# Feed-forward stage: the rows of z become bf16 whole numbers on ScalarE before TensorE transposes them

## The reference

```python
def h_bitlinear(x, w):
    xq = act_quant(fwht(x))      # Hadamard rotation, then each row rounded to whole numbers of 8 bits times its scale
    wq = weight_quant(w)         # weights rounded to -1, 0, 1 times one scale
    return jnp.einsum('bsh,oh->bso', xq, wq)
gate = h_bitlinear(hidden_states, w_gate)      # 512 -> 2048
up = h_bitlinear(hidden_states, w_up)          # 512 -> 2048
return h_bitlinear(jax.nn.silu(gate) * up, w_down)   # 2048 -> 512
```

## Time and profile before

| what | us |
|---|---|
| median of three executions | 3221.47 (3221.32 to 3223.74) |
| the profiled execution, device time | 3223.19 |
| its span in the profile | 3221.4 |
| step of the feed-forward loop | 20.80 |
| PE busy in one such step | 20.31 |
| ACT, DVE, POOL busy in one such step | 12.66, 14.13, 14.72 |

### The profile page before, as it was taken

The page is one execution under the profiler, slowest core; times in us unless marked ns, Lnnn a source line. Parts: engine busy times, 40 slices in busy tenths (PEclk is TensorE's granted clock), DMA queues, the critical chain, the costliest instruction groups (busy, mean ns, idle before and its releaser), DMA issues. The chain is left out here.

```text
span 3221.4 us, 66765 instructions
## 1 busy us (share of the span) xinstructions
PE 2801.9 (87%) x26968; PEld 1507.3 (47%) x26968; DVE 1976.9 (61%) x2992; ACT 1467.2 (46%) x2442; POOL 1016.9 (32%) x712
## 2 busy tenths in 40 slices
PE   6999999386888888888745999999999699999997
PEld 3444444143444444444422444444444366666665
DVE  3444444359978989789881444544452466666665
ACT  2222222375766766767612422222221365666565
POOL 0000000116627438347370000000000276677765
PEclk9999999687988988989865999999999899999999
DMA  6999898200000000000004032322210111111110
GB/s 240 332 331 326 290 332 286 91 14 1 2 28 9 22 28 2 28 23 7 15 14 164 14 116 79 118 79 100 97 47 7 63 40 36 39 39 39 39 36 30
DMA packets 126429, 290.27 MB, mean 90 GB/s; under 512 B 30496, under 2 KB 35360, under 8 KB 122112
## 3 DMA queue, kind: packets, MB, share of 16 engines
q1 hardware_dynamic: 122752, 261.91, 23.4%
q10 hardware_dynamic: 3456, 25.17, 2.4%
HBM read 245.02 MB, written 42.01 MB: 89 GB/s over the span
## 5 line engine op out<-in xcount | busy, mean ns | idle before, releaser
L814 POOL TENSOR_TENSOR b_tmp<-b_L,b_U 128x496 f32<-128x496 f32 (+30 forms) x248 | 253.2, 1021 | 510.8 <-ACT b_L L1058 492.0
L2017 POOL TENSOR_TENSOR d_zb<-d_za 128x1024 f32<-128x1024 f32 x32 | 75.5, 2358 | 1046.3 <-DVE d_za L2073 1046.3
L860 PE MATMUL b_e<-b_hT,b_wqkv 128*128 128x512 f16 x1152 | 285.6, 395 | 35.0 <-DVE b_hT L1241 24.0
L1302 DVE TENSOR_TENSOR b_U<-b_U,b_tmp 128x1488 f32<-128x1488 f32 (+30 forms) x248 | 283.1, 1141 | 8.6
L816 POOL TENSOR_TENSOR b_U<-b_U,b_tmp 128x496 f32<-128x496 f32 (+30 forms) x248 | 279.5, 1127 | 19.4
L1300 DVE TENSOR_TENSOR b_tmp<-b_L,b_U 128x1488 f32<-128x1488 f32 (+30 forms) x248 | 267.1, 1077 | 13.6 <-ACT b_L L1058 8.0
L1526 PE MATMUL c_r<-c_hT,c_g_pair 128*128 128x512 f16 x1056 | 254.1, 392 | 13.1 <-DVE c_hT L1691 13.1
L1700 DVE SCALAR_TENSOR_TENSOR c_av<-c_r,c_sg 128x512 f32<-128x512 f32 x88 | 60.9, 692 | 303.2 <-PE c_r L1526 246.7
L1526 PE MATMUL c_r<-c_hT,c_u_pair 128*128 128x512 f16 x1056 | 242.6, 379 | 0.0
L1526 PE MATMUL c_d<-c_d_pair,c_aT 128*128 128x512 f16 x1056 | 241.0, 379 | 0.0
L1882 PE MATMUL d_m<-s_region,d_xiT 128*128 128x512 bf16 x1024 | 228.2, 381 | 3.7 <-ACT d_xiT L1996 2.4
(11 more groups left out here) (236 smaller groups left out, 5600.3 us busy)
## 6 DMA issues: line engine op xcount, KB each, us to landing
a_cT<-in_ctxT SPq DMA_DIRECT2D x128, 512.0 KB, 9.6
a_cn<-in_ctx SPq DMA_DIRECT2D x128, 512.0 KB, 9.3
a_x_ln<-in_x SPq DMA_DIRECT2D x8, 1024.0 KB, 16.1
a_cw<-in_ctx SPq DMA_DIRECT2D x128, 64.0 KB, 9.8
a_x_res<-in_x SPq DMA_DIRECT2D x32, 256.0 KB, 11.2
x<-a_x_out SPq DMA_DIRECT2D x32, 256.0 KB, 10.9
b_xg<-x SPq DMA_DIRECT2D x8, 1024.0 KB, 5.4
om<-b_hT SPq DMA_DIRECT2D x32, 256.0 KB, 2.0
```

The lines of the kernel that those rows point to most:

```text
L814: nc.gpsimd.tensor_tensor(tmp[:, QV, s + 1:S, :], lo, us, ALU.mult).then_inc(pool_prod, 1)
L860: mm = pe.matmul(p[:], w_qkv[:, a, i, n, c * P:(c + 1) * P], hp[:, b, n, :], start=(n + a + b == 0), stop=(n == DC - 1 and a == 1))
L1302: V.tensor_tensor(U[:, 0:QV, s + 1:S, :], U[:, 0:QV, s + 1:S, :], tmp[:, 0:QV, s + 1:S, :], ALU.subtract).then_inc(sub, 1)
L2017: nc.gpsimd.tensor_tensor(o[:, :, 0, :], a[:, :, 0, :], a[:, :, 1, :], ALU.add).then_inc(bf, 1)
```

## The change

ACT gets a new instruction, `whole_z`, for each half of zs: it subtracts the constant and writes zq, bf16 whole numbers. The first stands ahead of xT in ACT's list, the second behind it. PE transposes zq in bf16 against a bf16 identity, eight pieces to a bank, so there are two banks zi0 and zi1 for a tile, and ACT copies each to ziT as one 128x1024 copy. The ring has four entries. The bf16 identity is made once by DVE.

```diff
+        zq = sb("zq", [P, W], BF16)
+        ident16 = sb("ident16", [P, P], BF16)
-        RQ = Ring(st, ["zi0", "zi1", "zi2", "zi3", "down", "pad"], 2, "q")
+        RQ = Ring(st, ["zi0", "zi1", "down", "pad"], 2, "q")
...
             def transpose_zi(i, hs):
                 for h in hs:
                     p, full = RQ.open(pe, i, f"zi{h}")
-                    pe.wait_ge(clip2, 2 * i + h // 2 + 1)
-                    for j in range(4):
-                        c = 4 * h + j
-                        mm = pe.transpose(p[:, j * P:(j + 1) * P], zs[:, c * P:(c + 1) * P], ident[:])
+                    p = p[:].bitcast(BF16)
+                    pe.wait_ge(zq_ready, 2 * i + h + 1)
+                    for j in range(WC // 2):
+                        c = WC // 2 * h + j
+                        mm = pe.transpose(p[:, j * P:(j + 1) * P], zq[:, c * P:(c + 1) * P], ident16[:])
                     mm.then_inc(full, 1)
...
+            def whole_z(i, h):
+                act.wait_ge(clip2, 2 * i + h + 1)
+                cols = slice(h * W // 2, (h + 1) * W // 2)
+                A.activation(zq[:, cols], zs[:, cols], ACT.Identity, bias=offset[:, 1:2]).then_inc(zq_ready, 1)
...
+                if do["end"]:
+                    whole_z(i, 0)
                 if do["two"]:
                     p, _ = RX.take(act, r, "xT")
                     RX.take(act, r, "had")
                     A.activation(xT[:, 0, :], p[:], ACT.Copy, scale=HS).then_inc(xT_hi, 1)
+                if do["end"]:
+                    whole_z(i, 1)
...
-                        for t in (2 * h, 2 * h + 1):
-                            p, free = RQ.take(act, i, f"zi{t}")
-                            A.activation(ziT[:, 4 * t:4 * t + 4, :].rearrange("p c n -> p (c n)"), p[:],
-                                         ACT.Identity, bias=offset[:, 1:2]).then_inc(free, 1)
+                        p, free = RQ.take(act, i, f"zi{h}")
+                        part = ziT[:, WC // 2 * h:WC // 2 * (h + 1), :]
+                        A.copy(part.rearrange("p c n -> p (c n)"), p[:].bitcast(BF16)).then_inc(free, 1)
```

More of the change, by code:

```diff
@@ L1814, in ffn_phase @@
         xT_hi, am, q1, xs_ready, clip1 = (sem(n) for n in ("xT_hi", "am", "q1", "xs_ready", "clip1"))
-        y_ready, zo_ready, first, bf, am2, q2, zs_ready, clip2 = (
-            sem(n) for n in ("y_ready", "zo_ready", "first", "bf", "am2", "q2", "zs_ready", "clip2"))
+        y_ready, zo_ready, first, bf, am2, q2, zs_ready, clip2, zq_ready = (
+            sem(n) for n in ("y_ready", "zo_ready", "first", "bf", "am2", "q2", "zs_ready", "clip2", "zq_ready"))
         dsc_ready, summed = sem("dsc"), sem("summed")
@@ L1852, in _ @@
         def _(pe):
+            pe.wait_ge(set_ready, 2)
             def transpose_x(i, r):
@@ L1913, in down @@
                 for c in range(WC):
-                    if c % 4 == 0:
-                        RQ.used(pe, i, f"zi{c // 4}")
+                    if c % (WC // 2) == 0:
+                        RQ.used(pe, i, f"zi{c // (WC // 2)}")
                     mm = pe.matmul(p[:], ziT[:, c, :], w_d[:, c, :], start=(c == 0), stop=(c == WC - 1))
@@ L1934, in body @@
                 if do["end"]:
-                    transpose_zi(k - 2, (0, 1))
+                    transpose_zi(k - 2, (0,))
                 if do["main"]:
@@ L1938, in body @@
                 if do["end"]:
-                    transpose_zi(k - 2, (2, 3))
+                    transpose_zi(k - 2, (1,))
                 if do["main"]:
@@ L1954, in _ @@
             A = nc.scalar
-            act.wait_ge(set_ready, 1)
+            act.wait_ge(set_ready, 2)
+            def whole_z(i, h):
+                act.wait_ge(clip2, 2 * i + h + 1)
+                cols = slice(h * W // 2, (h + 1) * W // 2)
+                A.activation(zq[:, cols], zs[:, cols], ACT.Identity, bias=offset[:, 1:2]).then_inc(zq_ready, 1)
             def body(k, do):
@@ L1961, in body @@
                     if not (isinstance(i, int) and i == 0):
-                        RQ.take(act, i - 1, "zi3")
+                        RQ.take(act, i - 1, "zi1")
                 for j in range(NB):
@@ L2026, in _ @@
             V = nc.vector
+            V.tensor_copy(ident16[:], ident[:]).then_inc(set_ready, 1)
             V.memset(offset[:, 0:1], LOW)
```

## The result

| | us |
|---|---|
| changed kernel, median of 4 | 3359.28 (3356.22 to 3361.34) |
| kernel before, median of 4 | 3222.60 (3221.32 to 3226.37) |
| ratio, 95% interval | 1.0421, 1.0408 to 1.0435 |
| span of the profiled execution after | 3359.5 |
| forecast | 3316, range 3230 to 3345 |

The kernel is slower by 4.2%, some 137 us. The direction was forecast and the time lies above the range.

A forecast was written before the change was run, and what follows sets the result against it. PE bounds the kernel at 20.80 us a step; after the change a ring through POOL, DVE and ACT does. 3223.2 + 70 (ring and last steps) + 25 (clock) = 3318 profiled, forecast 3316 us, range 3230 to 3345.

The forecast's parts named there:

- The gain on PE: Transposes of z on PE: 16 a step go to bf16 at 0.06 us each, saving 0.8 us a step, plus the bank wait.
- if nothing else moved: Loop step with only PE's savings counted: 20.80 - 1.45 = 19.35 us.
- What ACT gets: ACT's list: two `whole_z` at 1.05 and two copies at 0.93 us, 1.7 us more a step.
- The race with POOL: DVE's second clip against POOL's last pass: POOL goes first by 0.14 us, and the clip takes 2.91 us.
- The ring: Closed chain through POOL, DVE and ACT in the loop: 23.20 us a step, 2.40 over 20.80; 70 us with the last steps.
- Rival (a): DVE's second clip wins against POOL's last pass: step 21.12 us, time 3233 us; chance 12%.
- The clock: PE's granted clock falls behind a 3.8 us stall in the loop: 1.8 us in every second step, 25 us.
- every second: Share of the 28 loop steps in which PE's stall brings the low clock; no step to all steps as ends.
- The upper end of the range, every step at 1.8: Low clock on PE in all loop steps: 50 us, time 3341 us; the range ends at 3345.

The follow-up runs named there:

- The last experiment: Changed kernel with DVE's clip writing the bf16 whole numbers, no `whole_z` on ACT and the minimum left out: 3183.88 us, ratio 0.9877.
- The kernel before with the small copy: Kernel before plus one 128x128 copy ahead of xT on ACT: 3316.07 us; with POOL's sixth pass also waiting for the second clip: 3225.91 us.
- the one in which POOL yields: Changed kernel with POOL's sixth pass waiting until DVE's second clip is done: 3240.89 us, ratio 1.0062.
- the filled kernel: Changed kernel with 14 more PE matmuls a step, results dropped, where PE would stand: 3299.13 us, ratio 1.024.
- The filling experiments: Changed kernel with extra PE matmuls in the stall, results dropped: 14 a step, 3299.13 us; 5 a step, 3337.34 us.

## Why the prediction was right in its mechanism and wrong in its size

- **The gain on PE** was as forecast. Eight bf16 transposes are 0.45 us apart from the next group (2967.98 to 2968.43 above), 0.056 each, where the forecast took 0.06. The Trainium skill's 81 ns for such a pair (TensorE: Matmul & The Clock Gate, "Back-to-back issue gap") is not what these rows show. The last experiment, where ACT has no `whole_z`, has nearly the step that the forecast gave "if nothing else moved": 19.35 forecast, 19.45 in most steps.
- **What ACT gets.** `whole_z` takes 1.15 and gives way after 1.06 (1.05 forecast), the bf16 copy of 1024 columns takes 1.03. In the kernel with the second `whole_z` behind the copies yT such a copy is followed after 0.89 (2956.14 to 2957.03), 0.93 forecast. Right.
- **The race with POOL** was right in mechanism, place and nearly in margin: 0.14 us behind forecast, 0.11 measured. The kernel before with the small copy shows it without the change (92.5 us with the race open, 4.9 with it closed), and the one in which POOL yields shows the change without it. In the changed kernel the clip that lost ends at 2991.20, 0.56 behind POOL's pass (2990.64), and by itself it takes 0.69: it did its work when the pass was over. The Trainium skill's rule that the port is an exclusive lock for a whole instruction (SBUF — State Buffer, "SBUF: two separate sides") fits each of these rows.
- **The ring** was forecast at 23.20 us with the clock aside, and the filled kernel measured 23.34; 70 us forecast for it with the last steps, 75.6 measured (3299.13 against 3223.56). The 27 steps are 68.6 of it. Rival (a), DVE first, was forecast at 21.12 and 3233 us; the kernel in which POOL yields has 21.23 and 3240.89.
- **The clock** is the term that failed: "I take 1.8 us, near the row, in every second of 28 steps, 25 us". It was low in every step. The difference between the changed kernel and the filled one is 60.2 us, where the forecast had 25; 54 of it are in the 27 steps measured, 2.00 a step (25.34 less 23.34), and the rest is ahead of them and behind. The cost of one low stretch (1.8 forecast, 1.3 to 2.9 measured) was near; their number was half. The upper end of the range, every step at 1.8, was then too low as well, since in 11 of the 27 steps the slow work covers both groups of `rotate_y`: 3.75, 1.06 and 2.74 us in the step shown against 1.95, 0.61 and 1.95.
- The reason given for "every second" was that the stall has work close on both sides. The filling experiments do not bear it out: the stall has the same work on both sides in all of them, and with 0.9 us of it left the clock stays, with 2.75 it falls in 20 of 27 steps, with 3.8 in 27 of 27. Both stalls over 3 us in the earlier trace rows were followed by slow work; that should have been taken as the rule for one of 3.8.
- What stays open is in which steps a stall of 2 to 3 us brings the low clock. The kernel with the second `whole_z` moved has it behind 11 of 16 stalls of 1.9 to 2.0 us, and the kernel in which POOL yields never behind 1.78. No run separates the length of the stall from where it lies, nor, in the filling experiments, the shorter stall from the added work.

## What to carry to other kernels

Work moved to an engine with time to spare costs what is queued behind it: ask at each new wait which instructions of that engine stand behind, and who waits for them. Look in the timeline for two instructions that start within a tenth of a microsecond of each other on engines that share something: such a tie is held by nothing, a delay of 0.2 us elsewhere can turn it, and a wait that settles it costs little (4.9 us here, with the small copy). A stall of TensorE is to be priced twice, once for itself and once for the slow stretch behind it: in this loop in every step that had one of 3.8 us, in three of four at 2.7 to 2.8, in 11 of 16 at 1.9 to 2.0, in none at 1.8 or less.

## What the runs showed of the hardware that was not expected

- DVE's instruction of 128x1024 takes 0.69 us with a bf16 result, as with an f32 result, when POOL is idle; the 1.14 in the loop are a wait for POOL's fifth pass. It goes ahead of the sixth all the same, which it holds up (2.80).
- A copy of 128x128 on ACT, 0.27 us a step, made this kernel 3.0% slower.
- More matmuls made the program faster: 14 a step took 60 us off, 5 a step took 22 off.
